# Ternary stage of a four-stage network: the scale rows and two Hadamard stages earlier in the order, and the first batch's context loaded on its own

## What is computed

```
def act_quant(x):      # per token, 8 bit
    scale = 127.0 / clip(max(abs(x), -1), EPS);  return clip(round(x * scale), -128, 127) / scale
def weight_quant(w):   # ternary
    scale = clip(mean(abs(w)), EPS);             return clip(round(w / scale), -1, 1) * scale
def h_bitlinear(x, w): return act_quant(fwht(x)) @ weight_quant(w).T
gate, up = h_bitlinear(x, w_gate), h_bitlinear(x, w_up)      # 512 -> 2048
x = x + h_bitlinear(silu(gate) * up, w_down)                 # 2048 -> 512
```

## Time and profile before

| | |
|---|---|
| median of 3 runs | 1866.37 us (1864.92 to 1868.70) |
| the profiled execution: its time, its span | 1869.68 us, 1867.5 us |
| PE busy, weight loads | 1597.8 us (86%), 1048.2 us (56%) |
| DVE, ACT, POOL busy | 986.6, 704.3, 761.7 us |
| mean granted TensorE clock | 0.923 of full |

### The profile page before, as it was taken

One profiled execution on the slowest core, in us unless ns is written; L12 is line 12 of the kernel. 1 busy time (PEld: TensorE's weight loads), 2 busy tenths in 40 slices (PEclk: granted clock), 3 DMA queues, 4 the chain that ended last, 5 costly groups with the idle time before them and its releaser, 6 DMA issues. The chain is left out here.

```text
span 1867.5 us, 24292 instructions
## 1 busy us (share of the span) xinstructions
PE 1597.8 (86%) x8015; PEld 1048.2 (56%) x8016; DVE 986.6 (53%) x1648; ACT 704.3 (38%) x1141; POOL 761.7 (41%) x517
## 2 busy tenths in 40 slices
PE   4344288998987889999999875999999999999998
PEld 2222146464645433343333344878887888878876
DVE  2678678686857688978878723222221222222221
ACT  3443235354544457777767541111111111111111
POOL 1312253434355221243615547287076225361055
PEclk9666589999998879998989887999999999999999
DMA  8020498000002214443426034044144032322168
GB/s 306 1 90 1 157 386 302 1 1 1 1 1 74 72 42 116 125 135 99 134 70 200 15 115 160 24 170 158 34 163 164 28 120 77 128 98 78 34 113 203
DMA packets 90383, 195.88 MB, mean 105 GB/s; under 512 B 7105, under 2 KB 8514, under 8 KB 89666
## 3 DMA queue, kind: packets, MB, share of 16 engines
q1 hardware_dynamic: 71906, 157.07, 25.2%
q0 software_dynamic: 7168, 17.04, 4.0%
q10 hardware_dynamic: 11232, 20.77, 3.4%
HBM read 113.02 MB, written 81.32 MB: 104 GB/s over the span
## 5 line engine op out<-in xcount | busy, mean ns | idle before, releaser
L1541 DVE TENSOR_REDUCE neg_max<-psum 128x2 f32<-128x1024 f32 x256 | 300.9, 1220 | 53.6 <-PE psum L2038 52.6
L1127 ACT ACTIVATE probabilities<-psum 128x512 f32<-128x512 f32 x512 | 270.7, 601 | 104.4 <-PE psum L2065 100.4
L1659 DVE TENSOR_TENSOR expert_inner<-psum,expert_inner 128x512 f32<-128x512 f32 x78 | 54.0, 692 | 393.3 <-ACT expert_inner L1220 393.3
L2208 PE MATMUL psum<-expert_weight_parts,sorted_tokens_t_first 128*128 x624 | 250.8, 402 | 10.3 <-POOL expert_weight_parts L899 5.4
L2210 PE MATMUL psum<-expert_weight_parts,sorted_tokens_t_second 128*128 x624 | 246.9, 396 | 0.0
L2209 PE MATMUL psum<-expert_weight_parts,sorted_tokens_t_first 128*128 x624 | 246.7, 395 | 0.0
L1220 ACT ACTIVATE expert_inner<-psum 128x512 f32<-128x512 f32 x78 | 46.7, 599 | 401.3 <-PE psum L2210 401.3
L2065 PE MATMUL psum<-query_rows,key_rows 50*128 50x512 f32 x512 | 181.7, 452 | 6.9 <-ACT probabilities L1127 5.4
L2038 PE MATMUL psum<-key_rows,query_rows 48*128 48x512 f32 x512 | 175.2, 502 | 13.5 <-DVE neg_max L1541 11.1
L2076 PE MATMUL psum<-probabilities,value_and_one 128*32 128x512 f32 x1024 | 143.5, 634 | 0.0
L2208 PEld LDWEIGHTS psum<-expert_weight_parts,sorted_tokens_t_first 128*128 128x128 f32 x624 | 117.7, 189 | 42.2 <-issue 16.2
(11 more groups left out here) (271 smaller groups left out, 2997.0 us busy)
## 6 DMA issues: line engine op xcount, KB each, us to landing
sorted_x<-zero_rows SPq DMA_DIRECT2D x9, 3960.0 KB, 31.0
w_of_odd_expert<-in_L_ffn_w SPq DMA_DIRECT2D x8, 2048.0 KB, 9.1
wo_of_expert<-in_L_ffn_wo SPq DMA_DIRECT2D x7, 2048.0 KB, 9.1
query_rows<-query_rows_of_units SPq DMA_DIRECT2D x64, 192.0 KB, 3.6
w_of_even_expert<-in_L_ffn_w SPq DMA_DIRECT2D x6, 2048.0 KB, 11.9
sorted_tokens<-sorted_x ACTq DMA_DIRECT2D x39, 264.0 KB, 2.8
sorted_y<-expert_out ACTq DMA_DIRECT2D x39, 256.0 KB, 2.1
query_rows_of_units<-dims_first SPq DMA_DIRECT2D x32, 256.0 KB
```

Of the source, the lines that this page charges most:

```text
L1127: nc.scalar.activation(prob[t % 2][:, i * SEQ:(i + 1) * SEQ], bank[4 + n % 3], ACT.Exp, scale=HD ** -0.5).then_inc(c_e, 1)
L1541: nc.vector.tensor_reduce(of_pair[:, p, st, :], ring(("max", (m, i))).rearrange("p (h n) -> p h n", h=2), AX.X, ALU.max, negate=True).then ...
L1659: nc.vector.tensor_tensor(h, bank[2 * half + 1], h, ALU.mult).then_inc(e_h, 1)
L2208: nc.tensor.matmul(out_bank, hi[:, cols], w_r[:, bass.ds(w_at, 512)], start=start, stop=False)
```

## The change

- PE: `scales_spread(b + 1)` stands right behind `inner_rotated(b, 2, 3)`, ahead of tile 3. Before it stood behind `inner_rotated(b, 3, 1)`.
- ACT: `scale_rows_out(b + 1)` stands ahead of `rotated_rows(b, 3, 0)`, where before it was behind `scaled_inner(b, 2)`; `first_part(b, 3)` stands ahead of `rotated_rows(b, 2, 0)`.
- DVE: `second_stage(b, 2)` stands ahead of `inner_scales(b, 0)`, and `second_stage(b, 3)` ahead of `quantised_inner(b, 0)`. POOL's program is the same.
- SP: behind the clearing DMAs, and waiting for all ten of them, a new DMA loads the 512 rows of the first batch's context to a tile of its own, which lies over `zero_rows`. PE's first context chunk reads that tile and waits for that load; the load of all the context stays where it was, for the later batches and for the values.

```
+        ctx_first = Map(nc, small.at, small.end).tile("context_of_first_batch", [P, ST * CTX])
         zero_rows = small.tile("zero_rows", [P, WIDE])
...
+            sp.wait_ge(d_zf, 16 * (ZEROED + 1))
+            sp.dma_start(ctx_first[:].rearrange("p (t c) -> p t c", c=CTX),
+                         ctx_512[0].rearrange("(t p) c -> p t c", p=P)).then_inc(ld_ctx, 16)
             sp.wait_ge(b_up, BATCH * FC)
...
+                first_part(b, 3)
                 rotated_rows(b, 2, 0)
...
                 inner_transposed(b, 0)
-                first_part(b, 3)
                 scaled_inner(b, 1)
                 rotated_rows(b, 2, 2)
                 rotated_rows(b, 2, 3)
+                if more:
+                    scale_rows_out(b + 1)
                 rotated_rows(b, 3, 0)
                 inner_transposed(b, 1)
                 rotated_rows(b, 3, 1)
                 scaled_inner(b, 2)
-                if more:
-                    scale_rows_out(b + 1)
...
+                second_stage(b, 2)
                 inner_scales(b, 0)
-                second_stage(b, 2)
                 if more:
                     quantised_tokens(b + 1)
+                second_stage(b, 3)
                 quantised_inner(b, 0)
                 if more:
                     scale_diagonals(b + 1)
                     quantised_tokens_t(b + 1)
                 inner_scales(b, 1)
-                second_stage(b, 3)
                 quantised_inner(b, 1)
...
                 inner_rotated(b, 2, 3)
+                if more:
+                    scales_spread(b + 1)
                 inner_rotated(b, 3, 0)
                 inner_quantised_transposed(b, 1)
                 inner_rotated(b, 3, 1)
-                if more:
-                    scales_spread(b + 1)
                 down_projected(b, 1)
...
-                    pe.wait_ge(ld_ctx2, 16)
+                    pe.wait_ge(*((ld_ctx2, 16) if b else (ld_ctx, 32)))
...
-                    src = (ctx_c[:, (b * ST + t) * CTX:(b * ST + t + 1) * CTX] if chunk == CTX_CHUNK
+                    src = ((ctx_c if b else ctx_first)[:, (b * ST + t) * CTX:(b * ST + t + 1) * CTX] if chunk == CTX_CHUNK
```

## The result

The changed kernel takes 1838.94 us (median of 4 runs, 1835.87 to 1842.17), the kernel before on the same chip 1867.53 (4 runs, 1864.92 to 1870.81). The ratio is 0.9846, with a 95% interval from 0.9822 to 0.987: faster by 28.6 us, 1.5%. The forecast was 1852, a gain of 14.3, in a range from 1836 to 1863; the gain came out twice as large. The profiled execution took 1842.17 us with a span of 1840.0 and a mean granted clock of 0.928.

What follows compares the result with a forecast made beforehand. PE's work plus its waits bound each tail. Tails of 40.9 + 3.1 + 3.9 + 1.6 = 49.5 us gain 10.0, the entry 2.0, tail 3 2.3: 1866.37 - 14.3 = 1852 us, range 1836 to 1863.

Steps and rivals of the forecast that it cites:

- The waits taken away: Tails 0 to 2: PE's waits for the token scale rows, 16.5 us in three, go, with the slow matmuls behind them.
- The two-input instructions held by POOL: Tails: DVE instructions with two SBUF inputs stand still until POOL's running instruction ends; a new PE wait of 3.1 us follows.
- Step 1: Tail 0, DVE: tile 2's second stage, free at 293.25, waits for POOL to 295.50 and ends at 297.8.
- step 3: Tail 0, DVE: tile 0's scales start at 297.8, their maximum waits for POOL to 301.3, and they end at 302.3.
- steps 4 and 5: Tail 0: the next tokens wait for POOL to 303.7 and run to 305.1; PE gets a new wait of 3.1 us.
- the rival that nothing is held up: Tails: POOL starts later or DVE comes first, so no instruction waits; tails of 40.9 us, 1823 in all; chance 0.08.
- the third rival: Where the prediction speaks of the rule's absence: nothing is held up, tails of 40.9 us, 1823 in all; chance 0.08.
- The diagonals held: Tails 0 to 2: three of four token scale diagonals wait for two POOL halves, to 313.5; a PE wait of 3.9 us.
- the first rival: Tails: diagonals aren't held, or pass between POOL's halves; second wait some 0.6 us, tail 46.0, 1841.6 in all; chance 0.27.
- Step 6: Tail 0, ahead of tile 0's projection: diagonals held by POOL delay the copies to about 315.6; a second PE wait of 3.9 us.
- The entry and tail 3: Entry to the last tail: 2.0 us gained, bounds 2.0 and 4.3; inside tail 3: 2.3 us, bounds 0 and 2.8.
- The rivals that the gain is given back, or slower, by the clock: Tails: both new waits cost the full 2.6 us of clock, 1863, chance 0.09; or half the work runs slow, 1886, chance 0.06.

## Why the prediction was right in kind and short in size

- **The waits taken away, and that the gain reaches the end:** right. None for the token scale rows is left in the trace, and the move of the scales alone gives 25.1 us in the tails.
- **The two-input instructions held by POOL:** right, within 0.3 us. Step 1 said 3.4 us for the first half of the second stage (3.34), step 3 said 302.3 for the end of the scales (302.66, with a start 0.63 later), steps 4 and 5 a first wait of 3.1 (2.8 in each of the three tails). With it the rival that nothing is held up (1823) is out. The prediction calls that one the third rival where it speaks of the rule's absence; it is the second of its list.
- **The diagonals held (the forecast against the first rival):** right. Their row is 5.13; the same row is 0.86 where no POOL call is beside it and 5.16 in another place where one is. The time measured lies near the first rival's 1841.6, but its mechanism isn't what happened: the wait that it denied is there. A time near a rival's number is no evidence for the rival; the rows are. And the forecast's own mechanism had a range of 1845 to 1858, which the measured 1838.94 lies outside: it is within 1836 to 1863 only because that takes in the first rival, so the hit is in part luck. The Trainium skill (VectorE: DVE Perf Modes, "Mode 2×_2P") says that an instruction such as this, with a single fp32 source in SBUF, gets its two results a cycle by using both read ports. The trace of the changed kernel agrees in so far as the diagonals were held, with the 5.13; it doesn't show the ports.
- **The term that was mis-sized, second wait and clock added up.** Step 6 had 3.9 for the second wait and the sum put 1.6 for the lower clock on top. The runs show 3.16 where the clock stayed at 1.00 (tail 0 of the repeated profile), which is the wait by itself; the forecast's is 0.7 too large. And where the clock was low behind the first wait, the second wait was shorter by just that: 1.74 and 1.97 in tails 1 and 2, against 2.95 in tail 0, where the clock fell only behind it. The timeline of PE in tail 1:

```profile
398.73 1.89 PE L1871 MATMUL psum<-ident_bf,uantised_tokens_of_batch 128*128 128x128 bf16 x16 [2.83 <-DVE uantised_tokens_of_batch L1377]
409.63 3.61 PE L1935 MATMUL psum<-down_ternary_t,inner_quantised_t 128*128 128x512 bf16 x16 [1.74 <-DVE quantised_t L1383]
```

  The transposes take 1.89 there, 1.40 in tail 0, and the tail is as long as the one at full clock (46.65 and 46.60): DVE's copies end the wait at the same moment either way. Here slow matmuls ahead of a wait that another engine ends cost nothing. They cost only behind the last such wait, as in tail 0 of the first profile:

```profile
315.44 5.30 PE L1935 MATMUL psum<-down_ternary_t,inner_quantised_t 128*128 128x512 bf16 x16 [2.95 <-DVE quantised_t L1383]
```

  5.30 against 3.61, and the tail is 48.26. So the terms 3.1 + 3.9 + 1.6 = 8.6 should have read 2.8 + 3.0 + 0 (5.8, or 7.4 with the clock), 2.9 too much in two tails and 1.2 in one: 7.0 us of the 8.6 by which the sum fell short of 22.9.
- **The entry and tail 3:** 2.0 forecast, 2.64 measured; 2.3 forecast, 3.28 and 4.94 measured. The second is above my bound of 2.8. I had taken a quarter of all waits for POOL. Tail 3 of before had 2.1 of these and 1.3 for the quantised tile behind them, 3.4 together, of which 0.5 is left in one profile and none in the other. Most of the 1.5 by which the two profiles of tail 3 differ (56.16 and 54.71) is one projection of 16 at the lower clock (5.31 against 3.63) behind a wait for ACT of 1.97 that both kernels have.
- **The last 5 us:** the spans differ by 27.5, the forecast's stretches by 22.9 less the 0.63. The repeated profiles give 26.7 up to the attention's start and 28.8 in all. What lies behind is the attention's length, which moves by up to 14 us between profiles of one kernel (458.7 and 444.7 for the kernel with the stages in the last batch alone, on two chips). It has the same 2421 matmuls each time; PE's busy time and the granted clock differ. Why one execution gets 0.95 and another 0.93 there stays open. The two comparisons of medians (0.9846 and 0.9853) put the whole gain at 27 to 29 us; the repeated pair accounts for it by the tails and the entry but for 2 us.
- **The rivals that the gain is given back, or slower, by the clock:** out. The mean clock of tails 0 to 2, between 0.90 and 0.94 before, is 0.96 in them, and 1.00 in tail 0 of the repeated profile.

Put together by parts, the scales give 25.1, the context 2.65, and the stages 3.3 to 4.9 in tail 3 once the context is early (1.9 without it); in return they take back 2.1 to 3.8 in each earlier tail, 8.1 in the first profile and 6.4 in the repeated one. The change is a good one with a part in it that loses; with the stages moved where nothing held stands ahead of a reader, 42.0 us a tail is within 1.4 of PE's busy time.

## What to carry to other kernels

When two engines take turns at SBUF, an instruction's place is not only a place in its queue but a place beside the other engine's calls: lay the two timelines over each other, mark the calls that can't run together, and price a held instruction against everything queued behind it. When a sum adds a wait and a slower clock, ask who ends the wait: if it is another engine, the time that PE loses ahead of it is already in it. Try the parts of a combined change one by one, since one can carry the gain and another take some of it back; and profile an unchanged kernel twice before a remainder of a few us is given a cause.

## What the runs showed of the hardware

- VectorE and GpSimd pass the turn at the end of each instruction, not of each call. POOL's halves end at about 311.3 and 313.7. The stretch around the four diagonals, split near these ends, with the diagonals alone counted (length, DVE busy, in brackets how many of them fall in the window, one that spans two windows in both; then clock, DMA share, GB/s):

```profile
308.80:309.20 0.40, 0.37 (x2) 1.00 1.06 391
309.20:311.20 2.00, 2.00 (x1) 1.00 1.05 376
311.20:311.60 0.40, 0.40 (x2) 1.00 1.08 401
311.60:313.40 1.80, 1.80 (x1) 1.00 1.05 387
313.40:314.00 0.60, 0.56 (x2) 1.00 1.07 394
```

  One diagonal is held through the first half, ends as it ends, the next is held through the second half, and the last comes behind. The longest single one is 2.416 us, the shortest 0.273: a tiny instruction can cost a whole POOL half, and these four in a row cost two.
- What a held instruction loses doesn't go by its size but by where in POOL's instruction it falls. A maximum of 128x1 (0.16 alone) took 1.29, 1.28 and 1.27 us behind POOL's two-input halves, and 1.99 in tail 3 of the changed kernel, where it came 0.4 into a half. An instruction of POOL with one input holds too: in the repeated profile of the changed kernel, quantising 2048 elements started at 331.68 beside the normalisation (L731, about 2.07 an instruction) and took 1.45 in place of 1.23. That is not a milder hold. POOL's next instruction starts at 332.03, and the quantising ends 1.1 behind that, as it does behind the two-input calls; it came 0.35 before the end. POOL's next one took 3.04 in its turn.
- One case doesn't fit. The maximum has two inputs, and 0.38 into such a one-input instruction it took 0.39 to 0.40, far from its end; later in an instruction of the same form (L835, 0.74 behind its start) it took 0.16. Why it wasn't held to the end stays open.
- The lower clock comes behind PE waits of 2 to 3 us in some executions and not in others: tail 0 of the changed kernel had it at 0.96 in one profile and 1.00 in the next, with nearly the same two waits (2.79 and 2.95, 2.83 and 3.16).
